# Four-layer graph network: the second edge order made by a top-eight sort on VectorE, with fewer scatters

## The chip, the cores and the metric

One core of a Trainium2 chip. The metric is the device time of one execution in microseconds, the median of several runs. Engines by their short names: PE is TensorE, DVE VectorE, ACT ScalarE, POOL GpSimd, SP SyncE, which here issues plain DMAs only.

## What is computed

Four graph layers on 3125 nodes of 256 features (padded to 3200, 25 blocks of 128) and 103125 edges (padded to 128 partitions x 806), each layer added to x and followed by a layer norm. Cut to what matters:

```python
x = _layernorm(x + _L0_gnn_ref(x, edge_index, edge_attr_2, ...))
x = _layernorm(x + _L1_gnn_ref(x, W_self, W_neigh, src, dst))
x = _layernorm(x + _L2_gnn_ref(x, Wf, Wb, loop_weight, ..., src, dst, edge_type_16, 0, 0))
x = _layernorm(x + _L3_gnn_ref(x, edge_index, ...))
...
# in _L1_gnn_ref
h_sparse = _maxk(feat @ W_neigh, 32)
summed = segment_sum(h_sparse[src], dst, num_segments=n)
return feat @ W_self + summed / maximum(deg, 1.0)[:, None]
...
# in _L2_gnn_ref, for (src, dst) and again for (dst, src)
proj = einsum('ni,rio->rno', feat, W)
m = (proj[etypes, src_idx] + bias) * norm_per_edge[:, None]
m_out = segment_sum(m, dst_idx, num_segments=n)
...
# in gt_layer of _L3_gnn_ref, twice: rows are src, cols are dst
att = clip(einsum('ehd,ehd->eh', q, k), -10.0, 10.0)
attNorm = segment_sum(exp(att), rows, num_segments=n)[rows]
```

The edges come sorted by dst. Layers 0, 1 and the forward half of layer 2 sum over dst; the backward half of layer 2 and both attention passes of layer 3 sum over src, and need the edges in a second order, by block of src (src // 128).

## The kernel before

**Edge sums.** Edges stand in 832 tiles of 128 in SBUF, each tile with nodes of one block only: `slots_d` (by dst) and `slots_s` (by src, three words an edge: node, relation row, place in the block). Every pass over the edges takes the tiles in 208 groups of four. ACT writes the four columns of row numbers (`gidx`, four slots in a ring), POOL issues four indirect DMAs that gather 128 table rows each (`gather_loop`, L233), DVE writes the one-hot matrices (`one_hot`, L242), PE multiplies them by the rows (`sum_tile`, L273), and DVE adds the four results to the block's sums (`adder`, L261). ACT may write slot n only when the sums of group n - 4 are done, so POOL runs at most four groups ahead. Stages in order, with the names used here:

- e0, layer 0 (L558 to L648), then norm n0; d1, layer 1's dense part, with a top-32 of each row by MAX8 and MATCH_REPLACE8 (L1195, L1198) and table1 stored;
- e1, layer 1's edge sum, then norm n1; d2, the dense part of layer 2;
- pf, the projections of 16 relations to `table2f` (PE L1436, DVE L1284, SP stores L893); e2f, its edge sum, with the backward projections beside it (from `rel_res`, loaded by SP at its start, L816, in eight pairs);
- e2b over `slots_s`, then layer 3: e3a and e3b over `slots_s`.

**The second order.** A counting sort spread over the program. `sort_keys` (L396 to L406) forms keys and records before e0. In e0, DVE counts the edges of each block between groups (`count_bin`, L411), `sort_tiles` (L443 on) makes the block starts, and `rank_bin` (L418 to L425) gives the first 208 edge columns a row each, one block of src after every fourth group. In e1 the other 598 columns are ranked in the same way. The rows are then used by `scatter` (L500 to L513): POOL copies 13 columns of records and rows to a stage buffer, then issues 13 indirect DMAs, each writing 128 records of three words to `slots_s_dram`. 208 of the 806 scatters follow e0's gathers on POOL's queue, 598 follow e1's, ahead of e2f's:

```python
            gather_loop(pool, "e0", table0, 2 * ROW0)
            pool.wait_ge(sem("gs_rows"), 1)
            scatter(pool, "gs", slots_s_dram, rec_s, row_s, 0, NS_EARLY)
            ...
                gather_loop(pool, "e1", table1, C)
                pool.wait_ge(sem("gs_moved"), 1)
                pool.wait_ge(sem("gs_rows"), 2)
                scatter(pool, "gs", slots_s_dram, rec_s2, row_s2, NS_EARLY, NS)
                for s in range(2):
                    pool.wait_ge(sem(f"pf_stored{s}"), 32 * PAIRS * (NB // 5) // 2)
                gather_loop(pool, "e2f", table2f, C)
```

SP waits for all of them after six of the eight pairs of relation weights (L527) and loads `slots_s` back.

## Time and profile before

| | us |
|---|---|
| median of 3 runs (9871.92 to 9894.19) | 9883.51 |
| span of the profiled execution, first to last instruction | 7939.2 |
| busy: POOL / PE / DVE / ACT | 5744.1 / 4723.0 / 4571.4 / 1304.4 |
| mean granted TensorE clock, share of full | 0.790 |

The profile gives the profiled execution's span alone, not a time of its own with what lies around it; the runs' median is 1944.3 us longer than the span. A POOL indirect DMA is busy while POOL writes its descriptors; the data lands later.

### The profile page before, as it was taken

The page shows a single profiled execution, that of the slowest core. Times are in us where ns is not written, and L with a number is a line of the kernel's source. Part 1 is how long each engine was busy: PE and PEld are TensorE (multiplying, and loading weights), DVE is VectorE, ACT ScalarE, POOL GpSimd, SP SyncE. Part 2 cuts the span into 40 slices and gives each one's busy share as a digit, 9 for nine tenths or more (in the row PEclk, how much of TensorE's full clock was granted, in tenths as well). Part 3 has the DMA queues.
Part 4 walks back from the last instruction along what each step waited for, and adds up shares of the span by engine and source line. Part 5 has one row for each costly group of instructions (what it writes and reads, how often), then busy time and mean ns, then how long its engine had stood idle before and what let it go on. Part 6 is the DMA issues. An engine that isn't in the chain of part 4 may idle for free.

```text
span 7939.2 us, 105932 instructions
## 1 busy us (share of the span) xinstructions
PE 4723.0 (59%) x17448; PEld 3281.5 (41%) x17449; DVE 4571.4 (58%) x11380; ACT 1304.4 (16%) x5226; POOL 5744.1 (72%) x5938
## 2 busy tenths in 40 slices
PE   4555653355555890077777556655666665666664
PEld 3333431233333440044444334433555554555553
DVE  6788887355444440055555544444666666666666
ACT  4666650000000000000000000001211111111111
POOL 4777777777777777777777777774677774777773
PEclk7777676677777995599999776676888887888887
DMA  3332330233333351055555333332333333333332
GB/s 100 56 57 55 57 50 21 66 97 98 101 103 87 117 161 31 23 149 157 158 157 158 100 102 103 102 103 67 101 102 101 101 102 80 100 101 100 101 101 64
DMA packets 513845, 751.71 MB, mean 95 GB/s; under 512 B 232770, under 2 KB 365943, under 8 KB 513271
## 3 DMA queue, kind: packets, MB, share of 16 engines
q0 software_dynamic: 252096, 604.80, 28.1%
q1 hardware_dynamic: 261686, 146.25, 6.1%
q8 instruction: 18, 0.29, 0.0%
q14 instruction: 45, 0.36, 0.0%
HBM read 624.19 MB, written 126.41 MB: 95 GB/s over the span
## 4 chain that ended last, share of the span: by engine, by line
POOL 51%; issue 35%; DMA 5%; ACT 3%; DVE 2%; PE 2%; POOLq 1%; ACTq 0%; DVEq 0%; SPq 0%
POOL rows L233 41%; POOL slots_s_dram L513 10%; DMA rows<-table,gidx 3%; ACT msg L577 2%; PE ps L273 1%; ACT big L565 1%; PE ps L359 1%; DMA rows<-table2f,gidx 0%; DVE big L671 0%; DMA rows<-table3b,gidx 0%; DMA rows<-table3a,gidx 0%; POOLq L77 0%; DMA rows<-table2b,gidx 0%; DVE x_sb L680 0%; DVE acc L261 0%
## 5 line engine op out<-in xcount | busy, mean ns | idle before, releaser
L261 DVE TENSOR_TENSOR acc<-acc,ps 128x257 f32 (+3 forms) x4992 | 1879.7, 377 | 1980.8 <-PE ps L273 1788.6
L273 PE MATMUL ps<-rows,onehot 128*128 128x257 f32 (+1 forms) x4992 | 1689.7, 498 | 1664.6 <-DMA rows<-table2f,gidx 602.2
L273 PEld LDWEIGHTS ps<-rows,onehot 128*128 128x128 f32 x4992 | 1162.6, 244 | 2277.8 <-issue 1711.8
L233 POOL DMA_INDIRECT rows<-table,gidx x1664 | 1647.6, 990 | 512.7 <-issue 458.7
L273 PE MATMUL ps<-msg,onehot 128*128 128x136 f32 (+1 forms) x4992 | 1282.9, 418 | 536.9 <-ACT msg L577 345.6
L273 PEld LDWEIGHTS ps<-msg,onehot 128*128 128x128 f32 x4992 | 981.6, 253 | 835.1 <-issue 378.6
L233 POOL DMA_INDIRECT rows<-table3a,gidx x832 | 820.9, 987 | 362.4 <-issue 251.3
L233 POOL DMA_INDIRECT rows<-table3b,gidx x832 | 829.3, 997 | 333.2 <-issue 251.3
L233 POOL DMA_INDIRECT rows<-table2b,gidx x832 | 821.2, 987 | 269.1 <-issue 251.6
L513 POOL DMA_INDIRECT slots_s_dram<-stage,stage_row x806 | 798.7, 991 | 274.4 <-issue 226.9
L233 POOL DMA_INDIRECT rows<-table2f,gidx x832 | 788.6, 948 | 253.4 <-issue 253.4
L776 DVE TENSOR_TENSOR big<-ps,rows 128x512 f32<-128x512 f32 x416 | 287.8, 692 | 724.3 <-DMA rows<-table3b,gidx 363.4
L735 PE MATMUL ps<-ident,onehot 128*128 128x128 f32 x1664 | 310.2, 316 | 543.4 <-DVE onehot L242 538.1
L744 PE MATMUL ps<-acc,msg 128*128 x3328 | 564.6, 324 | 80.9 <-issue 78.0
L744 PEld LDWEIGHTS ps<-acc,msg 128*128 128x128 f32 x3328 | 517.6, 236 | 129.1 <-issue 127.9
L223 ACT ACTIVATE gidx<-slots_d 128x4 int32 (+1 forms) x416 | 85.9, 208 | 2851.2 <-PE ps L273 2851.2
L735 PEld LDWEIGHTS ps<-ident,onehot 128*128 128x128 f32 x1664 | 196.0, 153 | 627.3 <-DVE onehot L242 535.9
L242 DVE TENSOR_TENSOR onehot<-iota,slots_s 128x512 f32<-128x512 f32 x624 | 430.2, 690 | 0.7 <-DVE acc L1317 0.2
L577 ACT ACTIVATE msg<-big,msg 128x64 f32<-128x64 f32 x1664 | 419.8, 334 | 6.8
L703 ACT ACTIVATE gidx<-slots_s 128x4 int32 (+1 forms) x416 | 85.5, 206 | 1762.8 <-DVE msg L797 1762.8
L1436 PE MATMUL ps<-wring,big 128*128 128x512 f32 x800 | 346.5, 597 | 7.9 <-DMA wring<-in_rel_f 7.9
L1453 PE MATMUL ps<-big,xts 128*128 128x512 f32 x600 | 285.2, 598 | 22.3 <-ACT xts L1036 22.3
...
## 6 DMA issues: line engine op xcount, KB each, us to landing
...
table2b<-msg SPq DMA_DIRECT2D x200, 256.0 KB, 2.3
rows<-table,gidx POOLq DMA_INDIRECT x1664
slots_d<-recs_d SPq DMA_DIRECT2D x832, 2.5 KB
rows<-table2f,gidx POOLq DMA_INDIRECT x832
rows<-table2b,gidx POOLq DMA_INDIRECT x832
rows<-table3a,gidx POOLq DMA_INDIRECT x832
rows<-table3b,gidx POOLq DMA_INDIRECT x832
```

The source lines that it names most:

```text
L223: nc.scalar.activation(gidx[:, h, :], src_ap[:, :, word], ACT.Copy).then_inc(sem("row_numbers"), 1)
L233: nc.gpsimd.indirect_dma_start(out=rows[:, j, 0:width], out_offset=None, in_=table[:, :], in_offset=bass.IndirectOffsetOnAxis(ap=gidx[:, h ...
L242: nc.vector.tensor_tensor(onehot[:, h, :, :], bc(iota[:, :].unsqueeze(1), [P, G, P]), bc(loc, [P, G, P]), ALU.is_equal).then_inc(sem(of(s, ...
L261: nc.vector.tensor_tensor(acc[:, bass.ds(b * width, width)], acc[:, bass.ds(b * width, width)], ps[:, bank + k, 0:width], ALU.add).then_in ...
L273: nc.tensor.matmul(ps[:, bank + k, 0:width], onehot[:, h, k, :], rhs, start=True, stop=True).then_inc(sem(of(s, "tile_sum")), 1)
L513: nc.gpsimd.indirect_dma_start(out=dram_slots[:, :], out_offset=bass.IndirectOffsetOnAxis(ap=stage_row[:, h, k:k + 1], axis=0), in_=stage[ ...
L577: last = nc.scalar.activation(msgA[:, h, k, a * F0:(a + 1) * F0], ms0[:, h, k, 0:F0], ACT.Copy, scale=msgA[:, h, k, HEADS * F0 + a:HEADS * ...
L735: last = nc.tensor.transpose(ps[:, h % 2, k * P:(k + 1) * P], onehot[:, h, k, :], ident[:, :])
L744: last = nc.tensor.matmul(ps[:, 2 + h % 2, k * D:(k + 1) * D], oneT[:, h, k, :], q_sb[:, bass.ds(b * D, D)], start=True, stop=True)
L776: nc.vector.tensor_tensor(qk3[:, h, :, :], ps[:, 2 + h % 2, :].rearrange("p (g d) -> p g d", d=D), rows4[:, h, :, 0:D], ALU.mult).then_inc ...
L1436: last = nc.tensor.matmul(ps[:, m % 5, :], xt_all[:, k, m * P:(m + 1) * P], wring[:, s, k, :], start=(k == 0), stop=(k == 1))
L1453: last = nc.tensor.matmul(ps[:, 4 + q % 4, :], xts[:, 0, k * P:(k + 1) * P], rel_res[2 * q + k], start=(k == 0), stop=(k == 1))
```

## The change

The second order is made during e1. SP loads src, dst and edge type after layer 1's weights. DVE packs each edge in one 32-bit word (63 - block of src, dst, place, type; `pack_codes`), and takes the eight largest of a partition's 808 words at a time (`top_of`, `less_top`): three rounds in every four groups, 34 times, so that each partition's words are sorted by block. The sorted words are cut in 202 chunks of four; the words of chunks that mix blocks are sorted once more on their own, in 14 rounds (112 words). `count_codes` and `code_rows` compare all 202 chunks (and 112 singles) with the 25 blocks in one instruction each to count them and to look up their rows. POOL then places 202 chunks and 112 single words (the compiled program has 112, the change's name 104) in `codes`, right from SBUF. Before e2f, SP loads `codes` tile by tile, PE transposes seven pieces, and DVE decodes them to `slots_s`. The sort's work before and in e0 goes, with all scatters after e0.

```diff
+    CHUNK = 4
+    NCH = -(-EC // CHUNK)
+    SW = NCH * CHUNK
+    SORT_IT = -(-SW // 24)
+    NSG = -(-((BINS + 1) * CHUNK) // 8) * 8
+    SORTED = 24 * SORT_IT
+    COUNTED = -(-(4 * (SORT_IT + 1) + 2 + NSG // 8 + 2) // 4) * 4
     KD, KS = 5, 3
...
+        def pack_codes(dve, link):
+            dve.wait_ge(sem("gs_loaded"), 16 * 3)
+            flip = (FULL_KEY << 7) & ~(P - 1)
+            link(nc.vector.memset(left[:, EC:SW], LOWEST))
+            link(nc.vector.tensor_scalar(part_i, src_i, P - 1, 4, ALU.bitwise_and, ALU.logical_shift_left))
+            link(nc.vector.tensor_scalar(src_i, src_i, flip, flip, ALU.bitwise_xor, ALU.bitwise_and))
+            link(nc.vector.scalar_tensor_tensor(part_i, src_i, KEY_BIT - 7, part_i, ALU.logical_shift_left, ALU.bitwise_or))
+            link(nc.vector.scalar_tensor_tensor(part_i, dst_i, 12, part_i, ALU.logical_shift_left, ALU.bitwise_or))
+            link(nc.vector.tensor_tensor(left[:, 0:EC].bitcast(i32), part_i, et_i, ALU.bitwise_or))
+            dve.sem_inc(sem("gs_replaced"), 1)
...
+        def top_of(dve, r, steps):
+            after(dve, "gs_replaced", steps + 1)
+            dve.nop(nofuse=True)
+            nc.vector.max(top8[:, r, :], left).then_inc(sem("gs_top"), 1)
+        def less_top(dve, r, steps):
+            after(dve, "gs_top", steps + 1)
+            dve.nop(nofuse=True)
+            nc.vector.match_replace(left, top8[:, r, :], left, LOWEST).then_inc(sem("gs_replaced"), 1)
...
+        def count_codes(dve, bins, eq, counts, width, link):
+            link(nc.vector.tensor_tensor(eq, bc(iota[:, 0:NB].unsqueeze(2), [P, NB, width]),
+                                         bc(bins.unsqueeze(1), [P, NB, width]), ALU.is_equal))
+            link(nc.vector.tensor_reduce(counts[:, 0:NB], eq, AX.X, ALU.add))
...
+        def code_rows(dve, bins, eq, table, before, look, pos, junk, to, width, link):
+            link(nc.vector.tensor_tensor(eq, eq, bc(table[:, 0:NB].unsqueeze(2), [P, NB, width]), ALU.mult))
+            link(nc.vector.tensor_reduce(look, eq.rearrange("p s c -> p c s"), AX.X, ALU.add))
+            link(nc.vector.scalar_tensor_tensor(junk, bins, float(NB), to, ALU.is_ge, ALU.mult))
+            link(nc.vector.scalar_tensor_tensor(pos, bins, float(NB), before, ALU.is_lt, ALU.mult))
+            link(nc.vector.tensor_tensor(pos, pos, look, ALU.add))
+            link(nc.vector.tensor_tensor(to, pos, junk, ALU.add))
...
+        BATCH = 16
...
+        def place_codes(pool):
+            single_rows = codes.rearrange("r (w a) -> (r w) a", a=1)
+            for i in range(NCH + NSG):
+                n = i // BATCH
+                if i % BATCH == 0:
+                    after(pool, f"gs_placed{n % 2}", 16 * BATCH * (n // 2))
+                if i < NCH:
+                    rows_out, at, what = codes, to_c[:, i:i + 1], kept[:, i * CHUNK:(i + 1) * CHUNK]
+                else:
+                    j = i - NCH
+                    rows_out, at, what = single_rows, to_s[:, j:j + 1], singles[:, j:j + 1]
+                nc.gpsimd.indirect_dma_start(
+                    out=rows_out[:, :], out_offset=bass.IndirectOffsetOnAxis(ap=at, axis=0), in_=what, in_offset=None,
+                ).then_inc(sem(f"gs_placed{n % 2}"), 16)
+        def codes_placed(eng):
             for h in range(2):
-                sp.wait_ge(sem(f"{o}_placed{h}"), SC_EDGES * 8 * NS)
-            sp.dma_start(slots[:, :], dram_slots.rearrange("(p t) w -> p (t w)", p=P)).then_inc(sem(o + "_slots"), 16)
...
-            sp.wait_ge(sem("gd_done"), 1)
-            weight(key_i, edges(src), "gs_loaded")
-            weight(other_i, edges(dst), "gs_loaded")
-            weight(etype_i, edges(etype), "gs_loaded")
...
+                weight(src_i, edges(src), "gs_loaded")
+                weight(dst_i, edges(dst), "gs_loaded")
+                weight(et_i, edges(etype), "gs_loaded")
...
-                        slots_load(sp, "gs", slots_s_dram)
+                        codes_placed(sp)
+                        tiles = codes.rearrange("r w -> (r w)")[0:T * P].rearrange("(t p) -> t p", p=P)
+                        full_t = T // P * P
+                        weight(codes_t[:, 0:T // P, :], tiles[0:full_t, :].rearrange("(k t) p -> t k p", t=P), "codes_loaded")
+                        weight(codes_t[0:T - full_t, T // P, :], tiles[full_t:T, :], "codes_loaded")
...
                     pool.wait_ge(sem(f"gd_placed{h}"), SC_EDGES * 8 * NS)
             pool.sem_inc(sem("gd_scattered"), 1)
-            pool.wait_ge(sem("gs_keyed"), 1)
+            pool.wait_ge(sem("gd_done"), 1)
             pool.memset(acc[:, :], 0.0).then_inc(sem("acc_clear"), 1)
+            pool.wait_ge(sem("attr_ranged"), 1)
...
-            pool.wait_ge(sem("gs_rows"), 1)
-            pool.wait_ge(sem("gs_filled"), 16)
-            scatter(pool, "gs", slots_s_dram, rec_s, row_s, 0, NS_EARLY)
...
             if layers > 1:
+                pool.wait_ge(sem("e0_done"), 1)
+                pool.iota(to_c, [[P, NCH]], base=TRASH_C // CHUNK, channel_multiplier=1).then_inc(sem("gs_trash"), 1)
+                pool.iota(to_s, [[P, NSG]], base=TRASH_S, channel_multiplier=1).then_inc(sem("gs_trash"), 1)
                 pool.wait_ge(sem("d1_stored"), TABLE_STORED)
                 gather_loop(pool, "e1", table1, C)
-                pool.wait_ge(sem("gs_moved"), 1)
+                pool.wait_ge(sem("gs_filled"), 16)
                 pool.wait_ge(sem("gs_rows"), 2)
-                scatter(pool, "gs", slots_s_dram, rec_s2, row_s2, NS_EARLY, NS)
+                pool.nop(nofuse=True)
+                place_codes(pool)
...
-            sort_keys(dve, "gs", link)
-            dve.sem_inc(sem("gs_keyed"), 1)
...
-            for n in range(R):
-                step(n, n)
-            with dve.Fori(0, NB) as b:
-                for h in range(R):
-                    step(b * R + (R + h), h)
-                count_bin(dve, "gs", b)
-            count_bin(dve, "gs", NB)
-            sort_tiles(dve, "gs", link)
-            with dve.Fori(0, NB) as b:
-                for h in range(R):
-                    step(b * R + ((NB + 1) * R + h), h)
-                rank_bin(dve, "gs", b, EARLY, sem("gs_rank"))
-            rank_bin(dve, "gs", NB, EARLY, sem("gs_rank"))
...
                 dve.wait_ge(sem("block_ev"), first["d1"] + NB)
-                nc.vector.tensor_copy(rec_s2, rec_s).then_inc(sem("gs_moved"), 1)
...
+                pack_codes(dve, link)
...
+                def group(n, h, begin=plain, end=plain):
+                    later = not isinstance(n, int) or n > 0
+                    if later:
+                        add = adder(dve, "e1", block_d, n - 1, 0, C + 1)
+                        add(0)
+                    after(dve, "tile_sum", tiles0["e1"] + G * (n - R + 1))
+                    one_hot(dve, "e1", slots_d, KD, n, h)
+                    begin(n)
+                    if later:
+                        for k in range(1, G - 1):
+                            add(k)
+                    end(n)
+                    if later:
+                        add(G - 1)
+                for n in range(R):
+                    group(n, n)
+                with dve.Fori(0, SORT_IT) as i:
+                    for h in range(R):
+                        if h < 3:
+                            group(i * R + (R + h), h, lambda n: top_of(dve, h, i * 3 + h), lambda n: less_top(dve, h, i * 3 + h))
+                        else:
+                            group(i * R + (R + h), h)
+                            nc.vector.tensor_copy(kept[:, bass.ds(i * 24, 24)].rearrange("p (r w) -> p r w", r=3), top8[:, 0:3, :])\
+                                .then_inc(sem("gs_kept"), 1)
+                            dve.wait_ge(sem("gs_kept"), i + 1)
+                n = R * (SORT_IT + 1)
+                dve.wait_ge(sem("gs_replaced"), 3 * SORT_IT + 1)
...
+                mixed_chunks(dve, link)
+                n += 2
+                for k in range(NSG // 8):
+                    steps = 3 * SORT_IT + k
+                    group(n, n % R, lambda n: top_of(dve, 0, steps), lambda n: less_top(dve, 0, steps))
+                    nc.vector.tensor_copy(singles[:, k * 8:k * 8 + 8], top8[:, 0, :]).then_inc(sem("gs_kept"), 1)
+                    dve.wait_ge(sem("gs_kept"), SORT_IT + k + 1)
+                    n += 1
...
+                    .then_inc(sem("gs_ge"), 1)
+                group(COUNTED + 6, (COUNTED + 6) % R)
+                dve.wait_ge(sem("gs_trash"), 2)
+                code_rows(dve, bin_c, eq_c, tab_c, upto, look_c, pos_c, junk_c, to_c, NCH, link)
+                dve.sem_inc(sem("gs_rows"), 1)
+                group(COUNTED + 7, (COUNTED + 7) % R)
+                code_rows(dve, bin_s, eq_s, tab_s, iota[:, 0:NSG], look_s, pos_s, junk_s, to_s, NSG, link)
+                dve.sem_inc(sem("gs_rows"), 1)
...
+                for half in range(2):
+                    link(nc.vector.tensor_copy(block_s[0:1, half * (T // 2):(half + 1) * (T // 2)], ps[0:1, 6 + half, 0:T // 2]))
+                rest = -(-(COUNTED + 9) // R)
...
                 link(nc.vector.tensor_copy(deg.unsqueeze(2), a1[:, :, C:C + 1]))
                 link(nc.vector.reciprocal(small[:, 160:160 + NB], small[:, 160:160 + NB]))
                 link(nc.vector.tensor_tensor(a1[:, :, 0:C], a1[:, :, 0:C], bc(small[:, 160:160 + NB].unsqueeze(2), [P, NB, C]), ALU.mult))
                 link(nc.vector.tensor_tensor(x3, x3, a1[:, :, 0:C], ALU.add))
-                dve.wait_ge(sem("gs_moved"), 1)
-                for h in range(2):
-                    dve.wait_ge(sem(f"gs_placed{h}"), SC_EDGES * 8 * NS_EARLY)
                 norm_dve(dve, "n1", x3, C, 1e-5, link)
                 dve.sem_inc(sem("e1_done"), 1)
                     dve.wait_ge(sem(f"pf_stored{s}"), 32 * PAIRS * (NB // 5) // 2)
                 dve.sem_inc(sem("pf_done"), 1)
                 link(nc.vector.memset(acc[:, :], 0.0))
+                dve.wait_ge(sem("codes_turned"), 1)
+                loc_i, node_i, type_i = decoded
+                for a, b, bank in ((0, 512, 5), (512, T, 6)):
+                    raw = ps[:, bank, 0:b - a].bitcast(i32)
+                    link(nc.vector.tensor_scalar(loc_i[:, a:b], raw, 4, 2 * P - 1, ALU.logical_shift_right, ALU.bitwise_and))
...
```

POOL's program from the end of e1's gathers to the start of e2f's. Before (L233 is a gather, L505 and L508 the stage copies, L513 the scatters; ISA rows are waits):

```order
L233 DMA rows<-table,gidx 128x256 x16
L520 UNCONDITIONAL_BRANCH
L520 ISA
L505 ISA
L505 COPY stage<-msg 128x39
L508 ISA
L508 COPY stage_row<-msg 128x13
L510 ISA
L513 DMA slots_s_dram<-stage,stage_row 106624x3 x13
```

Now (L252 is a gather, L645 the scatters):

```order
L71 COMPARE_AND_BRANCH
L252 DMA rows<-table,gidx 128x256 x16
L645 DMA codes<-msg 56064x4 x202
L645 DMA codes<-msg 224256x1 x112
L252 DMA rows<-table2f,gidx 128x256 x16
L71 UNCONDITIONAL_BRANCH
```

The stage copies and two loops of 13 scatters, run 46 times in all, have become 314 single scatters in a row.

DVE in e1's loop, at the end of a turn of four groups. Before (L261 adds a tile's sum, L418 to L425 rank one block):

```order
L261 ISA
L261 TENSOR_TENSOR acc<-acc,ps 128x257
L71 REGISTER_ALU
L261 ISA
L261 TENSOR_TENSOR acc<-acc,ps 128x257
L418 ISA
L418 TENSOR_SCALAR big,cnt<-big,iota 128x598
L421 SCALAR_TENSOR_TENSOR big<-big 128x598
L423 REGISTER_ALU
L423 SCALAR_TENSOR_TENSOR big<-big,base 128x598
L425 TENSOR_TENSOR big<-big 128x598
```

Now, within one group (L261 writes the one-hots, L280 adds a sum, L514 and L520 are a round of the sort):

```order
L261 TENSOR_TENSOR onehot<-iota,slots_d 128x512
L65 ISA
L514 MAX top<-big 128x8
L65 REGISTER_ALU
L280 ISA
L280 TENSOR_TENSOR acc<-acc,ps 128x257
L65 REGISTER_ALU
L280 ISA
L280 TENSOR_TENSOR acc<-acc,ps 128x257
L520 MATCH_REPLACE big<-top,big 128x808
L65 REGISTER_ALU
L280 ISA
L280 TENSOR_TENSOR acc<-acc,ps 128x257
```

The ranking after every fourth group is gone, and MAX and MATCH_REPLACE over 808 words stand between the additions of three groups in four.

## Rows read from the trace of the kernel before

**Rows 1.** The page: the chain of work that ended last, by engine and by line.

```profile
POOL 51%; issue 35%; DMA 5%; ACT 3%; DVE 2%; PE 2%; POOLq 1%; ACTq 0%; DVEq 0%; SPq 0%
POOL rows L233 41%; POOL slots_s_dram L513 10%; DMA rows<-table,gidx 3%; ACT msg L577 2%; PE ps L273 1%; ACT big L565 1%; PE ps L359 1%; DMA rows<-table2f,gidx 0%; DVE big L671 0%; DMA rows<-table3b,gidx 0%; DMA rows<-table3a,gidx 0%; POOLq L77 0%; DMA rows<-table2b,gidx 0%; DVE x_sb L680 0%; DVE acc L261 0%
```

**Rows 2.** Busy time by stretch: stretch and length, engines, granted clock, DMA share and GB/s.

```profile
core 0: us, PE busy (x) PEld busy (x) DVE busy (x) ACT busy (x) POOL busy (x), PEclk, DMA share, GB/s
...
97.00:1165.00 1068.00, 616.30 (x1653) 417.06 (x1654) 868.17 (x2720) 678.09 (x2874) 808.72 (x833) 0.74 0.31 56
1165.00:1455.00 290.00, 83.85 (x180) 37.83 (x178) 164.17 (x480) 27.61 (x92) 219.12 (x241) 0.64 0.09 16
1455.00:2548.00 1093.00, 625.56 (x1648) 425.00 (x1648) 554.90 (x1164) 42.44 (x204) 839.60 (x834) 0.72 0.35 99
...
2640.00:2991.00 351.00, 345.13 (x799) 152.42 (x797) 138.47 (x200) 0.00 (x0) 261.22 (x307) 0.99 0.51 160
2991.00:3353.00 362.00, 0.00 (x0) 0.00 (x0) 6.25 (x2) 0.00 (x0) 268.90 (x315) 0.50 0.05 10
3353.00:4395.00 1042.00, 764.21 (x2438) 451.63 (x2439) 589.52 (x1227) 52.83 (x231) 788.61 (x832) 0.98 0.53 156
```

**Rows 3.** POOL in order of time at the handovers: start, duration, what, idle before.

```profile
1455.67 1.00 POOL L233 DMA_INDIRECT rows<-table,gidx  x1 [0.30 <-issue]
...
2547.00 0.94 POOL L233 DMA_INDIRECT rows<-table,gidx  x1 [0.30 <-issue]
...
3351.90 0.95 POOL L513 DMA_INDIRECT slots_s_dram<-stage,stage_row  x1 [0.30 <-issue]
3353.16 0.99 POOL L233 DMA_INDIRECT rows<-table2f,gidx  x1 [0.30 <-issue]
```

**Rows 4.** POOL by line: count, busy us, mean ns, idle before.

```profile
L513 POOL DMA_INDIRECT slots_s_dram<-stage,stage_row x806 | 798.7, 991 | 274.4 <-issue 226.9 <-POOL stage_row L508 47.5
L233 POOL DMA_INDIRECT rows<-table2f,gidx x832 | 788.6, 948 | 253.4 <-issue 253.4
```

**Rows 5.** DVE in order of time: end of layer 0, table 1 stored, projections stored.

```profile
1185.03 0.43 DVE L261 TENSOR_TENSOR acc<-acc,ps 128x260 f32 x1 [0.21 <-DVE acc L261]
...
1371.12 5.56 DVE L1213 MEMSET acc<- 128x6600 f32 x1 [3.30 <-issue]
...
2992.89 5.56 DVE L1297 MEMSET acc<- 128x6600 f32 x1 [7.02 <-issue]
```

**Rows 6.** POOL before its first gather.

```profile
91.83 5.60 POOL L977 MEMSET acc<- 128x6600 f32 x1 [80.55 <-DVEq L1114]
```

**Rows 7.** A stretch of layer 1 after its ranking, columns as in rows 2.

```profile
2100.00:2500.00 400.00, 236.50 (x627) 159.49 (x627) 171.94 (x391) 16.23 (x78) 304.98 (x313) 0.72 0.35 102
```

**Rows 8.** DVE by line and shape: count, busy us, mean ns, idle before.

```profile
L1195 DVE MAX8 top<-msg 128x8 f32<-128x256 f32 x75 | 32.1, 428 | 7.7
L1198 DVE MATCH_REPLACE8 msg<-top,msg 128x256 f32<-128x256 f32 x75 | 30.7, 409 | 0.5 <-issue 0.3
...
L411 DVE TENSOR_SCALAR_CACHE_REDUCE big<-big,iota 128x806 f32<-128x806 f32 x26 | 27.2, 1047 | 0.2 <-DVE big L411 0.2
L418 DVE TENSOR_SCALAR_CACHE_REDUCE big<-big,iota 128x598 f32<-128x598 f32 x26 | 21.6, 829 | 0.2 <-DVE big L425 0.2
```

**Rows 9.** POOL scatters beside MAX8 work of DVE, and beside its wide additions.

```profile
1251.06 0.96 POOL L513 DMA_INDIRECT slots_s_dram<-stage,stage_row  x1 [0.30 <-issue]
...
2561.79 6.73 POOL L513 DMA_INDIRECT slots_s_dram<-stage,stage_row  x1 [0.30 <-issue]
```

**Rows 10.** DVE beside that long scatter.

```profile
2560.86 6.82 DVE L1236 TENSOR_TENSOR acc<-acc,small 128x6400 f32<-128x6400 f32 x1
```

**Rows 11.** SP's queue after the projections, and what the DMA engines moved from 2990 to 3040.

```profile
2991.81 6.22 SPq L816 DMA_DIRECT2D big<-in_rel_b  x12
...
GB/s 199 8 84 139 348 373 356 354 349 351 261 13 1 1 1 0 1 1 1 1 1 1 1 1 1 1 1 1 1 0 1 1 1 1 1 1 1 1 1 1
```

**Rows 12.** PE by line: the transposes by the identity.

```profile
L735 PE MATMUL ps<-ident,onehot 128*128 128x128 f32 x1664 | 310.2, 316 | 543.4 <-DVE onehot L242 538.1 <-issue 5.2
```

375 lines of the change are left out of this document (236 added, 139 removed).

## The prediction

> **What bounds the kernel now.** First I read the page's chain of waits [rows 1]. POOL carries 51% of it, and the 35% called issue are nearly all the gaps between POOL's own instructions, so read them as POOL's too. By line it is the gathers, 41%, and the scatters of the second order, 10%. Then the busy times by stretch [rows 2]: in no stretch but the projections (2640 to 2991, PE 345 of 351 us) does another engine fill its time. In 2991 to 3353 PE is idle and DVE busy 6 of 362 us: everybody waits for POOL's scatters. In 1165 to 1455 DVE is done with layer 0 and the top-32 long before POOL is free. The handovers on POOL's queue give the exact times [rows 3]: the gathers of e1 run from 1455.67 to 2547.94, the 598 late scatters up to 3353, and only then e2f's gathers begin. Last I read what else had to be ready at those handovers [rows 5]: table 1 was stored at 1371.1, where the clearing of the sums is released, and the last projections at about 2991.4 (1.5 us before the second clearing, which waits for them and starts at 2992.89; SP's next load, behind the same wait, was issued just before the ones at 2991.81 [rows 11]). So POOL is late by 84.6 us at e1 and by 361.8 us at e2f. That is the reach of this change; what is beyond it belongs to the gathers.
>
> **The change, part by part.** The sum is made against the profiled span, 7939.2 us. The runs' median is 9883.5, 1944.3 us more; I take that difference as fixed, and come back to it as a rival.
>
> *Before e0.* POOL's first gather waits for its clearing of the sums, which waited till 91.83 for the keys of the second order [rows 6]. Now it waits for the first order only, done some 12 us earlier by the three loads and seven DVE instructions that go (SP's loads of those words no longer stand ahead of the record loads either): -12, with bounds of -5 (only DVE's work goes) and -13.
>
> *e0.* 832 gathers take from 97 to 1165, 1.28 us each. DVE is busy 868 of 1068 us and loses about 27 us of counting (26 of 1.05 us [rows 8]) and the ranking of 208 columns. POOL's own pace hardly depends on it: I take 7 us for the stop at `sort_tiles` and small waits (0 to 15). DVE's last sum stands at 1185.0 [rows 5], 20 us after the last gather, part of it behind the last ranking: -5 (0 to -10).
>
> *Early scatters.* 208 scatters go. What is late next is table 1: the dense part and top-32 are a chain of their own from the end of e0. So e1's gathers start when the table is stored: -84.5. The bound on the other side is -80, if three more SP loads of 400 KB delay the weights.
>
> *e1.* The gathers took 1092.3 us. After its ranking POOL does 313 in 400 us [rows 7], 1.278 each, so 832 would be 1063. Into this DVE now gets 116 rounds of the sort. The shapes of 598 and 806 columns [rows 8] differ by 1.05 ns an element; MAX8 of 256 takes 428 ns and MATCH_REPLACE8 409, so 808 elements make 1.01 and 0.99 us, with 0.1 for loading the eight values 2.1 us a round. DVE's busy time after the ranking is 172 us in 400, 2.2 a group; with a round 4.3 us, and a group has 5.1. It fits, and since the order of additions is kept and POOL may run four groups ahead, I cost the sorting loop at nothing. The work at its end doesn't fit: compares and look-ups over 5050 and 2800 elements, by the wide addition of 6400 in 6.82 us [rows 10] 5.4 and 3.0 us each, four pairs of them in all, with small operations 10.8, 6.0, 12.5 and 7.3 us, and 5 us for the block tables, between seven groups or so. DVE behind by L gains back 1.6 us a group; POOL's lead forgives about 9. Going through them in order, 4, 6 and 6 us are left over: +17. Bounds are 0 and all 42. e1 is then 1080 us, -12 (from -50, at e2f's pace of 1042 for 832 [rows 2] and no stall, to +13).
>
> *Late scatters.* 598 scatters took 805 us, 1.345 each with the copies. The new 314 need no copies: 0.96 + 0.30 us [rows 9] = 1.26, or 397 us, and the two wide additions of the norm, beside which the one at 2561.79 took 6.73 instead of 0.96, add 11.5: 408 us. From the end of e1's gathers to the projections' store are 443.5 us. The cover is the projections, PE-bound and untouched. Even at the old 1.345 + 11.5 the 314 end in 434. So the scatters cost nothing, and e2f starts with the projections: -361.8.
>
> *Before e2f.* New in front of DVE's first one-hot: `codes` comes behind 12 weight loads, which keep the DMA engines at some 350 GB/s till 3003 [rows 11], so about 3005; seven transposes at two instructions of 0.316 us [rows 12] under 4.5 us; nine decodes of 2496 + 2496 elements at 1.05 ns and some 0.15 each, 6.6 us. DVE begins near 3015, not 2998. POOL meanwhile issues its four groups (20 us) and would stand from 3011 to about 3020: +9 (0 to +25). The last four weight loads wait behind the codes, but are needed eight groups later.
>
> Sum: -12 - 7 - 5 - 84.5 - 12 - 361.8 + 9 = **-473.3**, a span of 7466 and a time of 9410. All bounds on one side give 9349 and 9475.
>
> **A rule against the rows.** The scatter at 2561.79 was held for as long as an addition of two SBUF operands ran [rows 9, 10], while scatters beside MAX8 took 0.96 [rows 9]; I price the four wide compares as such holds, partly hidden in the 17 us. The Trainium skill ("SBUF — State Buffer", Who interferes with whom) says that tensor_tensor takes only the shared pair's read side, which descriptor writing does not need, though it holds up GpSimd instructions that read SBUF; an indirect DMA reads its row numbers there. By its first half the compares would cost POOL nothing and the placing 11.5 us less: by that rule e1 would be some 5 us shorter, and the hidden placing would only be better hidden. That sentence moves the sum to 9405 and no chance.
>
> **The rivals.**
>
> *The sort makes DVE the bound of e1* (0.11). If MAX8 and MATCH_REPLACE8 grow in proportion to width, a round is (428 + 409 + 92) x 808/256 = 2.9 us and a group 5.1, its whole period: then nothing is gained back, the 42 us of bursts show in full and each round costs perhaps 0.4 more, 46 us. 25 + 46 more than my 17: 9481. For it speaks that only one width of both is in the trace; against it that their 428 and 409 ns are what an addition of 256 takes, and that one grows by 1.05 ns an element.
>
> *The scatter of four costs like four* (0.02), the case slower than before. If POOL wrote a descriptor per word, 202 x 4 + 112 = 920 at 1.26 us and 11.5 make 1173 us against 443.5: 730 us more than the sum, a time of 10140. The point from which the change loses is a placing of 443.5 + 473 = 917 us, or 3.8 us for a scatter of four. Against it: a gather of 256 words takes 948 ns and a scatter of three words 991 [rows 4]; width has no price there.
>
> *What lies around the span scales with it* (0.06). Then the time falls by 473.3 x 9883.5 / 7939.2 = 589, to 9294. Nothing in the profile shows what the 1944 us are; work outside the first and last instruction has no reason to know of scatters.
>
> *The change doesn't do what it says, or another wait takes its place* (0.03): the placing waits for its own completions every 16 scatters, or the rows of the chunks come too late. At 1.8 us each it takes 577 us, 133 more than the cover: 9543.
>
> **How the numbers follow.** My case has the remaining 0.78, the forecast is its sum, 9410. Its own bounds are 9349 to 9475, and the first rival lies at 9481. A range of 9355 to 9505 holds both but for their tails, and leaves out the far cases (0.11), which is within 2 in 10. Faster by over 0.2% (20 us, what a measurement here can tell from no change) is all but the slow rival: 0.97; slower 0.02, same 0.01.
>
> **What would show it.** In the profile after: the first gather near 86; e1's first gather right at the clearing of the sums, near 1347; 808-wide MAX8 near 1.0 us, e1's gathers in 1065 to 1100 us with the loss in one place, at the wide compares; 314 scatters in about 408 us, the last one some 35 us before the projections' last store; e2f's first gather near 2871, with one stand of POOL of about 9 us after 16 gathers; everything after it unchanged, 4595 us from that gather to the end (4586 before, and that stand). I am wrong if the scatters of four are longer than those of one, if DVE has no idle time in e1, if PE idles between projections and e2f by more than 30 us, or if the time falls by a different amount than the span.

## The result

The kernel after takes 9426.88 us (median of 4 runs, 9384.17 to 9436.32), before 9877.88: a ratio of 0.953 [0.951, 0.955], 451 us less. Forecast were 9410 and a range of 9355 to 9505. The number is close; the working is not. The first line of the profile after says so:

```profile
span 9434.5 us, 105027 instructions
## 1 busy us (share of the span) xinstructions
PE 5082.2 (54%) x17459; PEld 3439.7 (36%) x17460; DVE 4737.4 (50%) x11500; ACT 1337.1 (14%) x5226; POOL 5238.6 (56%) x5323
...
another core or an unknown queue 11%; PE 10%; issue 5%; DVE 5%; DVEq 2%; POOL 1%; DMA 0%; ACT 0%; SPq 0%; POOLq 0%; ACTq 0%
```

This execution took 9436.32 us, so only 1.8 us lie outside its span. I had put 1944 us there. And POOL, 51% of the chain before [rows 1], has 1% of it now. That is not the change's doing: a profile of the kernel before with a time near 9870 (the next section) gives POOL 0%. The shares of such a chain add up to a third of the span only, so I read nothing else from it. The stretches between POOL's handovers, from the windows of the profile after (columns as in [rows 2]):

```profile
core 0: us, PE busy (x) PEld busy (x) DVE busy (x) ACT busy (x) POOL busy (x), PEclk, DMA share, GB/s
86.62:1480.10 1393.48, 582.15 (x1638) 401.98 (x1638) 811.76 (x2517) 683.03 (x2872) 816.67 (x832) 0.71 0.23 43
1480.10:1682.80 202.70, 82.70 (x185) 36.93 (x185) 158.97 (x486) 28.88 (x97) 0.47 (x3) 0.72 0.10 27
1682.80:2996.60 1313.80, 710.59 (x1672) 362.98 (x1672) 742.04 (x1491) 42.45 (x204) 821.23 (x832) 0.68 0.29 83
2996.60:3421.30 424.70, 63.96 (x160) 41.98 (x158) 61.57 (x160) 17.81 (x55) 320.65 (x314) 0.52 0.03 3
3421.30:3795.60 374.30, 346.37 (x800) 153.00 (x800) 140.32 (x206) 0.00 (x0) 0.04 (x1) 0.96 0.45 152
3795.60:9434.50 5638.90, 3263.52 (x12830) 2418.53 (x12830) 2766.06 (x6542) 540.63 (x1893) 3266.03 (x3328) 0.72 0.30 90
```

Row 1 is e0: 832 gathers in 1393 us, 1.68 us each, though POOL is busy as long per gather as before (816.67 / 832 = 0.98 us). Rows 4 and 5 are the surprise: the 314 scatters take 424.7 us, about the 408 forecast, but beside them TensorE is busy 64 us and not one of the 800 products of the projections is made. They all follow in row 5, in 346 us. The scatters were placed under a cover, and the cover all but stopped while they ran. The clock is not the reason: TensorE's granted clock was 0.52 in row 4, near the lower of its two levels (1.2 GHz), but it sat idle for 361 of the 424.7 us.

### The profile page after: what moved, and what is told of

The parts are those of the page before. It is cut to its first block and busy times, and to the rows that moved or that the text cites. A ratio compares the mean times of both kernels' runs of the same rounds, so it can differ in the third digit from the quotient of the medians.

```text
span 9434.5 us, 105027 instructions
## 1 busy us (share of the span) xinstructions
PE 5082.2 (54%) x17459; PEld 3439.7 (36%) x17460; DVE 4737.4 (50%) x11500; ACT 1337.1 (14%) x5226; POOL 5238.6 (56%) x5323
## 5 line engine op out<-in xcount | busy, mean ns | idle before, releaser
L280 DVE TENSOR_TENSOR acc<-acc,ps 128x257 f32 (+3 forms) x4992 | 1884.2, 377 | 2387.9 <-issue 1012.9
L292 PE MATMUL ps<-rows,onehot 128*128 128x257 f32 (+1 forms) x4992 | 1866.5, 513 | 1547.1 <-DVE onehot L261 624.1
L252 POOL DMA_INDIRECT rows<-table,gidx x1664 | 1637.9, 984 | 1212.2 <-issue 505.1
L292 PEld LDWEIGHTS ps<-rows,onehot 128*128 128x128 f32 x4992 | 1097.9, 244 | 2374.3 <-issue 1289.7
L292 PEld LDWEIGHTS ps<-msg,onehot 128*128 128x128 f32 x4992 | 1039.2, 269 | 1087.1 <-issue 905.1
L252 POOL DMA_INDIRECT rows<-table2f,gidx x832 | 796.0, 957 | 855.3 <-DMA table2f<-big 374.3
L252 POOL DMA_INDIRECT rows<-table3a,gidx x832 | 823.5, 990 | 690.2 <-ACT gidx L827 308.6
L252 POOL DMA_INDIRECT rows<-table3b,gidx x832 | 823.5, 990 | 650.9 <-ACT gidx L827 288.0
L252 POOL DMA_INDIRECT rows<-table2b,gidx x832 | 823.0, 989 | 443.3 <-issue 255.6
L868 PE MATMUL ps<-acc,msg 128*128 x3328 | 643.7, 355 | 469.4 <-issue 265.3
L868 PEld LDWEIGHTS ps<-acc,msg 128*128 128x128 f32 x3328 | 580.3, 262 | 532.9 <-issue 532.5
L859 PE MATMUL ps<-ident,onehot 128*128 128x128 f32 x1664 | 385.0, 375 | 699.4 <-DVE onehot L261 598.6
L261 DVE TENSOR_TENSOR onehot<-iota,slots_s 128x512 f32<-128x512 f32 x624 | 431.1, 691 | 553.4 <-remote 494.8
L859 PEld LDWEIGHTS ps<-ident,onehot 128*128 128x128 f32 x1664 | 268.9, 193 | 761.6 <-DVE onehot L261 522.6
L378 PE MATMUL ps<-wring,xts 128*128 128x256 f32 (+4 forms) x550 | 214.0, 518 | 365.6 <-issue 300.0
L645 POOL DMA_INDIRECT codes<-msg x314 | 320.7, 1021 | 104.0 <-issue 103.7
L1650 PE MATMUL ps<-big,xts 128*128 128x512 f32 x600 | 329.8, 678 | 83.9 <-ACT xts L1163 74.0
L1625 PE MATMUL ps<-wring,big 128*128 128x512 f32 x800 | 346.4, 596 | 23.4 <-DMA wring<-in_rel_f 23.4
```

The lines of the kernel that those rows point to most:

```text
L252: nc.gpsimd.indirect_dma_start(out=rows[:, j, 0:width], out_offset=None, in_=table[:, :], in_offset=bass.IndirectOffsetOnAxis(ap=gidx[:, h ...
L261: nc.vector.tensor_tensor(onehot[:, h, :, :], bc(iota[:, :].unsqueeze(1), [P, G, P]), bc(loc, [P, G, P]), ALU.is_equal).then_inc(sem(of(s, ...
L280: nc.vector.tensor_tensor(acc[:, bass.ds(b * width, width)], acc[:, bass.ds(b * width, width)], ps[:, bank + k, 0:width], ALU.add).then_in ...
L292: nc.tensor.matmul(ps[:, bank + k, 0:width], onehot[:, h, k, :], rhs, start=True, stop=True).then_inc(sem(of(s, "tile_sum")), 1)
L378: last = nc.tensor.matmul(ps[:, 2 + j, 0:wide], xts[:, j, k * P:(k + 1) * P], weights[:, k, 0:wide], start=(k == 0), stop=(k == kin - 1))
L645: nc.gpsimd.indirect_dma_start(out=rows_out[:, :], out_offset=bass.IndirectOffsetOnAxis(ap=at, axis=0), in_=what, in_offset=None,).then_in ...
```

## The experiments

### The kernel before, once more

Unchanged, to have a profile of an execution whose time is known. 

> The kernel before, unchanged, to get a profile of an execution whose time is known. Theory A (the missing 1944 us lie inside the loops; the profile shown of before was of a quicker execution): the span is the time less about 2 us, near 9876, with e0's gathers at about 1.68 us each and e2f's at about 1.54, as in the profile after, and the stage d2 slow as there (about 380 us). Theory B (they lie outside the span): a span near 7939 beside a time near 9880, e0 at 1.28 and e2f at 1.25 us a gather. If A holds, this run also gives the two stands before e1 and before e2f in such an execution; theory A1 has them at about 85 and 362 us as in the profile before, theory A2 (d2 is slow too, so that the projections end some 800 us after e1) has the second near zero, and most of the 451 us must come from somewhere else.

Measured: 9870.62 us (before in this series, with the next two runs: 9873.01), the profiled span 9848.0. Windows of its profile:

```profile
97.70:1499.40 1401.70, 557.32 (x1640) 383.26 (x1641) 878.28 (x2701) 679.82 (x2865) 811.28 (x833) 0.72 0.23 43
1499.40:1874.20 374.80, 98.18 (x193) 43.01 (x191) 162.85 (x495) 30.06 (x101) 216.89 (x240) 0.60 0.06 12
1874.20:3119.60 1245.40, 644.88 (x1652) 397.45 (x1652) 570.85 (x1165) 42.44 (x204) 831.20 (x832) 0.67 0.31 87
3119.60:3966.10 846.50, 248.17 (x375) 101.96 (x374) 98.02 (x215) 17.81 (x55) 602.01 (x690) 0.55 0.08 18
3966.10:4230.00 263.90, 255.56 (x588) 112.41 (x588) 104.70 (x152) 0.00 (x0) 0.00 (x1) 0.98 0.49 164
```

Theory A holds: 1.8 us lie outside the span, and every stretch up to e2f's first gather is longer than in [rows 2]. The three stretches without gathers that come later (e2f to e2b, e2b to e3a, e3a to e3b) are not: 15.4, 110.2 and 79.4 us here, 16.0, 109.3 and 80.0 in the profile that I worked from. From e1's last gather to e2f's first are 1110.4 us, not 805, and after the scatters TensorE still has 588 of its 800 products to do. Neither A1 nor A2 foresaw this.

### The kernel before without its 806 scatters

```diff
-            scatter(pool, "gs", slots_s_dram, rec_s, row_s, 0, NS_EARLY)
...
-                scatter(pool, "gs", slots_s_dram, rec_s2, row_s2, NS_EARLY, NS)
...
```

> The kernel before without its 806 scatters of the second order (208 after e0, 598 after e1) and without the waits for them; sorting and ranking stay. It leaves out the placing of the second order, so e2b and the attention layers gather row 0 throughout. Theory 1 (what POOL stands for after e0 and after e1 is worth what the profile before shows): 85 + 362 = 447 us less than before, about 9431, up to the start of e2f's gathers, and later stages may differ by gathering one row. Theory 2 (in an ordinary execution the second layer's dense part is so slow that the late scatters are nearly hidden already): e2f's first gather comes only some 100 us earlier. Theory 3 (the scatters themselves slow the dense part and the others beside them): more than 447 us, since the dense part gets back to 50 us.

Measured: 9144.48 us, 0.926 [0.925, 0.928], 729 us less. The two stretches of its profile:

```profile
1499.40:1705.50 206.10, 84.52 (x193) 38.09 (x193) 164.70 (x502) 29.74 (x101) 0.00 (x0) 0.72 0.08 20
2949.30:3391.60 442.30, 385.17 (x973) 182.58 (x972) 203.57 (x374) 17.39 (x55) 0.04 (x1) 0.93 0.40 131
```

Theory 3. Without scatters the second stretch is 442.3 us, what I had worked out for it (443.5). So 208 early scatters cost 374.8 - 206.1 = 169 us of the 298 they take, and 598 late ones 1110.4 - 442.3 = 668 of 846. Later stages gather one row over and over here and are slower for it (e2b 1378 us in place of 1242).

### The kernel after with its scatters issued twice

```diff
...
                 place_codes(pool)
+                codes_placed(pool)
+                place_codes(pool, 1)
```

> The kernel after with its 314 scatters issued twice, the second time after the first has landed. In its profile POOL stood 374 us between the last scatter and the projections. Theory 1 (the placing is hidden work with 374 us to spare, and does nothing to others): the second pass takes 425 us and 5 us of waiting, so 56 us more, about 9483. Theory 3 (the scatters slow the dense part of layer 2, which took 381 us beside them and ended with them): the dense part and the projections after it move little if it would have ended anyway at 3436, again about 56 us more; but if the projections are slowed as well, 100 to 400 us more.

Measured: 9806.14 us, 379 more than after. Windows:

```profile
3040.00:3855.00 815.00, 189.91 (x298) 81.98 (x298) 84.04 (x193) 17.80 (x55) 616.51 (x594) 0.54 0.07 13
3855.00:4164.40 309.40, 285.86 (x652) 125.04 (x652) 115.77 (x168) 0.00 (x0) 0.00 (x0) 0.96 0.45 153
```

The 374 us of POOL's idle time are no reserve. The second pass of some 430 us moves e2f's first gather 369 us later, since beside it TensorE makes only 800 - 652 = 148 products of the projections, 65 us' worth at the speed of the second row. So the projections are held up as well, the case for which 100 to 400 us more were expected.

### A memset in place of each scatter, and scatters from 32 partitions

```diff
-                nc.gpsimd.indirect_dma_start(
-                    out=rows_out[:, :], out_offset=bass.IndirectOffsetOnAxis(ap=at, axis=0), in_=what, in_offset=None,
-                ).then_inc(sem(f"gs_placed{n % 2}"), 16)
+                nc.gpsimd.memset(slots_s[:, 1000:2160], 0.0).then_inc(sem(f"gs_placed{n % 2}"), 16)
+                after(pool, f"gs_placed{n % 2}", 16 * (BATCH * (n // 2) + i % BATCH + 1))
```

> The kernel after with each of its 314 placing scatters replaced by a memset of 128 x 1160 on POOL, about 1 us each, and a wait for it. It leaves the placing of the second order out (codes keep their filling, so e2b and the attention gather row 0). The question is what of the scatters slows the layers' dense part and the projections beside them: in the runs so far the stretch from e1's last gather to e2f's first takes 799 us with 314 scatters, 442 without any. Theory W (the writing of descriptors, or their DMAs, holds up TensorE): 442 us, so about 9070. Theory B (POOL being busy at all, for 400 us, holds up the others): 799 again, about 9430.

```diff
-                    rows_out, at, what = codes, to_c[:, i:i + 1], kept[:, i * CHUNK:(i + 1) * CHUNK]
+                    rows_out, at, what = codes, to_c[0:32, i:i + 1], kept[0:32, i * CHUNK:(i + 1) * CHUNK]
```

(and the same for the single words). 

> The kernel after with its 314 scatters writing the rows of 32 partitions only, a quarter of the descriptors each. It leaves out three quarters of the placing. Theory W1 (the hold grows with descriptors or with POOL's time in the instruction): the scatters take less than their 0.97 us, 0.4 to 0.6, and the stretch from e1's last gather to e2f's first falls from 799 to about 442 + 357/4 to 442 + 357/2, 530 to 620 us. Theory W2 (each indirect DMA costs the others the same, whatever its size): about 800 again. Theory 0 (the DMA engines' small writes are the hold): they are a quarter, so about 530, with scatters as long as before.

Measured: 9286.58 and 9392.22 us, on another chip, where before takes 9829.99. The stretch from e1's last gather to e2f's first decides. With memsets, first their line in the profile (ns: least, median, most), then the windows:

```profile
L645 POOL MEMSET slots_s<- x314: 1065/1065/1117, 2938.5 to 3310.4; 128x1160 f32 x157
...
2938.50:3311.50 373.00, 300.10 (x776) 145.28 (x777) 193.56 (x322) 17.40 (x55) 334.63 (x315) 0.90 0.35 116
3311.50:3400.40 88.90, 82.05 (x192) 36.02 (x190) 33.59 (x49) 0.00 (x0) 0.02 (x2) 0.98 0.47 161
```

With scatters from 32 partitions:

```profile
L645 POOL DMA_INDIRECT codes<-msg x314: 856/865/6667, 2955.2 to 3370.4; - x157
...
2954.90:3371.30 416.40, 53.92 (x124) 32.63 (x125) 60.56 (x144) 13.44 (x40) 314.78 (x315) 0.50 0.03 3
3371.30:3766.50 395.20, 358.55 (x849) 162.24 (x847) 148.39 (x230) 4.14 (x15) 0.01 (x1) 0.95 0.43 144
```

POOL busy for 335 us with memsets leaves TensorE 300 us of work in 373, and the stretch is 461.9 us. Indirect DMAs of a quarter of the rows take 0.87 us in place of 0.97 and leave it 54 us in 416; the stretch is 811.6. So theory W, in the form W2: what holds the others up comes with the indirect DMA, not with POOL's work, and hardly depends on how many rows it moves. Its price is (811.6 - 442.3) / 314 = 1.18 us each. With 128 rows it is (799.0 - 442.3) / 314 = 1.14 on the first chip; on this one the next two runs have stretches of 808.2 and 809.4 us, 1.17 each. In time the whole for memsets misses its 9070, since e2b and the attention gather one row (e2b 1426 us).

### The large sort ahead of e1

```diff
+                with dve.Fori(0, SORT_IT) as i:
+                    for h in range(R):
+                        if h < 3:
+                            top_of(dve, h, i * 3 + h)
+                            less_top(dve, h, i * 3 + h)
...
                 with dve.Fori(0, SORT_IT) as i:
                     for h in range(R):
...
-                            group(i * R + (R + h), h, lambda n: top_of(dve, h, i * 3 + h), lambda n: less_top(dve, h, i * 3 + h))
+                        group(i * R + (R + h), h)
```

> The kernel after with the 102 rounds of the large sort (MAX8 and MATCH_REPLACE8 of 808) run in one piece ahead of e1's first group on DVE, no longer inside its groups. In the runs so far e1's gathers take 1314 us with the sort inside and 1245 without. Theory S (the rounds inside the loop cost the 69 us, since DVE's part of each group is on the ring of waits, while the bursts at the wide compares cost little): the rounds alone take 102 x 2.1 = 214 us ahead, and the groups then run at 1.497 us a gather, so e1 ends 214 - 69 = 145 us later, less four groups' lead: 9550 to 9575. Theory L (the 69 us are the wide compares, look-ups and the 14 small rounds, and the 102 rounds cost nothing inside): 200 to 215 us more, 9630.

Measured: 9559.91 us, 0.973 [0.971, 0.976] of before. Its windows, POOL's stand during the sort and then e1 with POOL's lead used up:

```profile
1649.80:1893.20 243.40, 4.83 (x11) 3.87 (x12) 208.31 (x335) 0.21 (x1) 0.00 (x0) 0.50 0.00 1
1893.20:3120.50 1227.30, 651.62 (x1652) 374.22 (x1650) 539.56 (x1131) 42.22 (x203) 807.48 (x816) 0.67 0.31 87
```

From e1's first gather to its last are 1491.3 us (1629.3 to 3120.5); with the sort inside, the three other runs on this chip have 1308.3 to 1324.4. The rounds alone take 247 us (1640.3 to 1887.2), not 214, and moving them costs 167 to 183, so inside the loop they had cost 64 to 80. That is theory S, with the rounds mis-sized. That the time falls in its range is luck: the range was built on the first chip's 9427 us, and on this one a kernel as fast as after takes 9375 (the next run).

### e2b on eight PSUM banks

```diff
-                    sum_tile(pe, s, n, h, k, 0, G, width, rows[:, h * G + k, 0:width])
+                    wide = s == "e2b"
+                    sum_tile(pe, s, n, h, k, h % 2 * G if wide else 0, 2 * G if wide else G, width, rows[:, h * G + k, 0:width])
...
-                    add = adder(dve, s, block, n - 1, 0, width)
+                    add = adder(dve, s, block, n - 1, (h + 1) % 2 * G if s == "e2b" else 0, width)
...
```

> The kernel after with e2b's sums on all eight PSUM banks in turn (banks 0 to 3 for even groups, 4 to 7 for odd) in place of four, so that TensorE may start a group's sums before VectorE has added the last ones'. Theory R (in ordinary executions the gather loops are bound by a ring of waits TensorE - VectorE, lengthened by TensorE's late ends beside POOL's indirect DMAs; 1.497 us a gather where POOL alone would need 1.25 to 1.30): e2b's pace falls to 1.30 to 1.40, 80 to 165 us less, 9260 to 9345. Theory P (POOL's own issue or the landing of the gathered rows bounds the loop): no change beyond 20 us.

Measured: 9374.69 us, 0.954 [0.952, 0.956], as after's 0.953. e2b's gathers take 1229.0 us; with four banks on this chip 1224.7 (the run with 32 partitions) and 1228.4 (sort first). Theory R falls for e2b, the one loop tried: its slower pace does not hang on the banks.

### Three runs that met a quick chip

The next three ran on a chip where the kernel before takes 7941.46 us (7935.36 to 7950.64, 7 runs). That is the kind of execution that the profile before shows. None of them could therefore decide between its theories.

```diff
...
-                        out=rows[:, j, 0:width], out_offset=None, in_=table[:, :],
+                        out=row_tile(h, k)[:, 0:width], out_offset=None, in_=table[:, :],
...
```

(`row_tile` gives the second four groups' rows from `msg`; e2b's loops count modulo eight, and its index waits for the sums of eight groups back.)

> The kernel after with e2b's ring of gathered rows eight groups deep in place of four (the other four in msg, which is free there), everything else of e2b as it was. Eight PSUM banks in place of four changed nothing (e2b 1.478 us a gather before and after). Theory K (late ends of TensorE's products and late register instructions on VectorE, up to 1.4 us each in the trace, are jitter that four groups of lead, 20 us, do not cover): with eight groups POOL hardly waits, 1.28 to 1.35 us a gather, 100 to 165 us less than after. Theory V (the held VectorE sequencer is itself the bound of e2b: its mean need of a group is already 5.9 us): no change beyond 20 us, whatever the ring.

Measured: 7467.03 us, 0.940 of before; e2b 1074.9 us, where the profile of before that I worked from has 1074.3.

```diff
                 pool.wait_ge(sem("gs_rows"), 2)
+                pool.wait_ge(sem("d2_done"), 1)
```

> The kernel after with POOL's 314 scatters held till the dense part of layer 2 is done (one wait more), so that they run beside the projections only. In the runs so far 424 us of scatters let the dense part (50 us alone) just finish. Theory C (what is held is the handing over between engines: the dense part passes each block through TensorE, ScalarE and back, the projections are long runs of products): the projections advance at 30% or more beside the scatters, so that the stretch from e1's last gather to e2f's first is 92 + 424 + 0.7 x 345 minus what ends later, 700 to 760 us in place of 799. Theory E (TensorE's own work is held, whatever it is): the projections advance at some 15 to 25%, 92 + 424 + 260 to 290 = 776 to 806, no gain beyond 25 us.

Measured: 7519.35 us, 0.947 of before. From e1's last gather to e2f's first are 496.6 us, the dense part's 85 and then the scatters' 412. Nothing is held up here, and so neither C nor E is tested. On such a chip the late start costs 37 us (459.5 without it, in the section after this one).

```diff
-                nc.gpsimd.indirect_dma_start(
-                    out=rows_out[:, :], out_offset=bass.IndirectOffsetOnAxis(ap=at, axis=0), in_=what, in_offset=None,
-                ).then_inc(sem(f"gs_placed{n % 2}"), 16)
+                wide = CHUNK if i < NCH else 1
+                first_row = TRASH_C // CHUNK + i * P if i < NCH else TRASH_S + (i - NCH) * P
+                nc.gpsimd.dma_start(rows_out[first_row:first_row + P, 0:wide], what).then_inc(sem(f"gs_placed{n % 2}"), 16)
```

> The kernel after with each of its 314 indirect scatters replaced by an ordinary DMA of the same 128 pieces to fixed rows, still issued by POOL. It leaves the placing out (the words go to rows that nothing reads). Theory W3 (it is the descriptors that POOL writes for an indirect DMA that hold up the others): the stretch from e1's last gather to e2f's first falls to 442 to 500 us unless POOL writes these descriptors too, which would show as about 1 us of POOL's time each. Theory D (the small writes to HBM themselves hold up the others): the stretch stays near 799 us though POOL's time for each falls.

Measured: 8437.19 us. POOL issues an ordinary DMA in 0.54 us and is done with all after 201, yet the stretch is 481 us, 22 more than with the indirect ones on a chip of this kind; no run says why. Whether ordinary DMAs hold the others up on a slow chip stays open. The long time is that of e2b, e3a and e3b, each gathering one row: 1380, 1384 and 1387 us for 1074, 1078 and 1081.

### The kernel after on the quick chip

Unchanged, and beside it the deeper ring again. 

> The kernel after, unchanged. The chips of this study are of two kinds: on two of them the kernel before takes 9830 to 9878 us, on a third 7941, as in the execution whose profile the prediction was made from. Theory Q (on the third kind the prediction's sum of stages holds as it was made, since the scatters hide there): if this chip is of that kind, 7466 us within 10, a ratio of 0.940, with 450 to 455 us from e1's last gather to e2f's first. If it is of the slow kind: a ratio of 0.951 to 0.955 and about 800 us there.

> The kernel with e2b's ring of gathered rows eight groups deep, again, beside the kernel after. On the quick chip POOL's own issue bounded e2b (1.29 us a gather) and the deeper ring gave nothing. Theory K (on a slow chip the holds are jitter that a lead of four groups does not cover): on a slow chip e2b falls from about 1.49 to 1.28 to 1.35 us a gather, 100 to 165 us less than the kernel after. Theory V (VectorE's held sequencer is itself the bound there): less than 20 us. On a quick chip: within 10 us of the kernel after.

Measured: 7484.63 us against before's 7943.82, 0.9421 [0.9405, 0.9437]; the deeper ring 7478.79. The chip is of the quick kind, and theory Q misses its own bounds there, if by little: 7484.63 for 7466 within 10, and 459.5 us from e1's last gather to e2f's first for 450 to 455. The deeper ring's e2b takes 1074.0 us, as after's does, as expected of a quick chip; K against V stays untried on a slow one. Windows of after on this chip, stretch for stretch as above:

```profile
86.70:1130.90 1044.20, 600.03 (x1644) 405.97 (x1645) 796.60 (x2529) 678.02 (x2876) 790.89 (x832) 0.76 0.32 57
1130.90:1332.90 202.00, 85.60 (x181) 37.98 (x179) 155.08 (x473) 27.63 (x92) 0.47 (x2) 0.70 0.11 27
1332.90:2417.50 1084.60, 625.63 (x1664) 420.82 (x1664) 730.19 (x1490) 42.45 (x204) 820.93 (x832) 0.71 0.36 100
2417.50:2841.50 424.00, 362.79 (x910) 173.02 (x910) 190.09 (x350) 17.41 (x55) 316.01 (x314) 0.92 0.52 125
2841.50:2877.00 35.50, 26.59 (x58) 11.13 (x56) 10.95 (x17) 0.00 (x0) 0.00 (x0) 0.89 0.60 154
2877.00:7483.70 4606.70, 2972.42 (x12830) 2184.74 (x12830) 2724.94 (x6542) 514.99 (x1893) 3262.25 (x3328) 0.84 0.38 110
```

Row 4: the same 314 scatters in the same 424 us, and TensorE busy 363 of them where it was 64. This is the cover that I had counted on. The dense part shows the difference in single instructions. VectorE's timeline on the slow chip (start, us, and the idle time before with what ended it):

```profile
3057.21 0.29 DVE L1432 COPY big<-xts 128x256 f32<-128x256 f32 x1 [8.46 <-remote]
3057.42 0.42 DVE L1434 SCALAR_TENSOR_TENSOR big<-ps,bias 128x256 f32<-128x256 f32 x1
3057.87 0.43 DVE L1437 TENSOR_TENSOR x_sb<-x_sb,big 128x256 f32<-128x256 f32 x1
3073.30 0.29 DVE L1432 COPY big<-xts 128x256 f32<-128x256 f32 x1 [15.00 <-remote]
```

and on the quick one:

```profile
2473.70 0.29 DVE L1432 COPY big<-xts 128x256 f32<-128x256 f32 x1 [0.77 <-PE ps L378]
2473.91 0.42 DVE L1434 SCALAR_TENSOR_TENSOR big<-ps,bias 128x256 f32<-128x256 f32 x1
2474.36 0.42 DVE L1437 TENSOR_TENSOR x_sb<-x_sb,big 128x256 f32<-128x256 f32 x1
2474.79 0.35 DVE L1432 COPY big<-xts 128x256 f32<-128x256 f32 x1
```

The instructions are as long; a block of the dense part comes every 10 to 17 us in place of every 1 or 2. In the gather loops the same shows in the register instructions of VectorE's queue. The line of the waits in e2b, on the slow chip (ns: least, median, most):

```profile
L65 DVEq ALU_OP  x927: 1/40/1402, 5203.1 to 6298.8; - x186
L65 DVEq EVENT_SEMAPHORE  x557: 1/21/1399, 5200.3 to 6298.2; - x186
```

and on the quick one:

```profile
L65 DVEq ALU_OP  x978: 40/40/40, 4000.1 to 4999.7; - x196
L65 DVEq EVENT_SEMAPHORE  x586: 21/21/21, 4001.2 to 4999.9; - x196
```

Equal medians, but some of them take 1.4 us where all took 40 or 21 ns.

## Why the prediction was near, and where it was wrong

The terms against both kinds of chip, in us. "Slow" is the kernel after less before in the profiles shown (9434.5 - 9848.0), "quick" after on the quick chip less the profile that I worked from (7483.7 - 7939.2):

| term | forecast | quick | slow |
|---|---|---|---|
| before e0 | -12 | -10.9 | -11.1 |
| e0's gathers | -7 | -23.4 | -8.2 |
| e0's last gather to e1's first | -89.5 | -88.4 | -172.2 |
| e1's gathers | -12 | -7.7 | +68.4 |
| e1's last gather to e2f's first | -361.8 | -345.7 | -311.4 |
| after that | +9 | +20.7 | +20.9 |
| sum | -473.3 | -455.5 | -413.6 |

By medians the slow chips' saving is 451; the 413.6 come from two single executions, before's at the quick end of its runs (9849.82, median 9870.62) and after's the longest of its four.

**The step that failed first** is "I take that difference as fixed". The 1944 us between span and median were not around the kernel but in it: the profile came from a quick chip, the times from a slow one. The rival that looked at this (0.06) let them scale with the span; it fell too, for they are not spread evenly either. What should have made me stop is that a profile and a time 25% apart are two different executions, and a sum made in one is not owed to the other. A sign that I had named came true: the time fell by another amount than the span, which rose from 7939.2 to 9434.5 us while the time fell by 451.

**The scatters cost nothing** was nearly right on the quick chip. The last one ended 35.5 us before e2f's first gather (forecast 35), but both sides of that were 16 us longer than forecast: all 314 took 424 us (408), and the cover 459.5 (443.5). In the cover it was the projections: 359 us from the first product's start to the last's, 346 in the kernel before, with TensorE waiting 8.7 us for VectorE where it had not waited at all, and busy 351.2 for 346.5. No run shows what held VectorE. On the slow chip they cost 357 of their 424.7 us. There my term -361.8 became -311.4, as two errors cancel: the old 598 cost 668 us there, not 362, and the new 314 cost 357, not 0. "Untouched" was the wrong word for the projections.

**Early scatters**: -84.5, or -89.5 with the tail of e0, came out on the quick chip at -88.4. On the slow one 208 of them held up the dense part and the top-32 as well: -172.2. **e0's gathers** were mis-sized: they lost 23.4 us there, for a forecast of 7 and a bound of 15.

**The sort in e1**: MAX8 and MATCH_REPLACE8 of 808 take 996 and 984 ns (forecast 1.01 and 0.99 us), so the first rival's proportional growth is out. The lines of VectorE in e1 on the quick chip:

```profile
L514 DVE MAX8 top<-big 128x8 f32<-128x808 f32 x116 | 115.5, 996 | 0.0
L520 DVE MATCH_REPLACE8 big<-top,big 128x808 f32<-128x808 f32 x116 | 114.2, 984 | 0.0
...
L579 DVE TENSOR_REDUCE big<-big 128x202 f32<-128x5050 f32 x1 | 9.0, 9007 | 0.0
```

One price was wrong, that of the look-up that sums the far axis: 9.0 us for 5.4 over 5050 elements, 4.8 for 3.0 over 2800. e1 took 1084.6 us there (forecast 1080). On the slow chip it took 68.4 more instead of 12 less. That is the first rival's outcome (its 46 us) by another way: not through longer instructions. The run with the sort ahead puts 64 to 80 us on the rounds, enough for all of the 68; that the delays in VectorE's queue leave no room for them in a group is my reading of the lines above, and no run tested it.

**The wide operations** held POOL as the rows before said. POOL's instructions and, below them, VectorE's beside them, on the quick chip:

```profile
2152.92 5.24 POOL L252 DMA_INDIRECT rows<-table,gidx  x1 [0.30 <-issue]
...
2432.02 6.67 POOL L645 DMA_INDIRECT codes<-msg  x1 [0.30 <-issue]
2439.00 6.55 POOL L645 DMA_INDIRECT codes<-msg  x1 [0.30 <-issue]
...
2151.93 5.41 DVE L550 TENSOR_TENSOR big<-iota,big 128x5050 f32<-128x5050 f32 x1
...
2431.02 6.83 DVE L1411 TENSOR_TENSOR acc<-acc,small 128x6400 f32<-128x6400 f32 x1
2437.88 6.82 DVE L1412 TENSOR_TENSOR x_sb<-x_sb,acc 128x6400 f32<-128x6400 f32 x1
```

Each held DMA ends some 0.8 us after VectorE's operation does, near the 0.95 us that one takes undisturbed. (L1411, like L1236 in [rows 10], which the forecast calls an addition, is a product.) Beside the reduction of 9.0 us (2203.23 to 2212.24) POOL's gathers kept to 0.95. The forecast's choice of the rows over a rule of the Trainium skill ("SBUF — State Buffer", Who interferes with whom) stands: that page infers that tensor_tensor takes only the read side of the shared pair and so leaves descriptor writing alone, and these indirect DMAs were held all the same. The page's other rule, that an operation with two inputs in SBUF holds up GpSimd instructions that read SBUF, would fit them, since they read their row numbers there; no run here tells whether it is that read that waits.

**Before e2f** POOL stood 12.1 us after its first 16 gathers (9 forecast), with all that comes after it 11.7 more than the 4595 given.

One reading was too strong and no term hangs on it: the 35% called issue [rows 1] are not nearly all gaps between POOL's instructions, which add up to 1693 us, 21% of the span.

That the total landed near 9410 on a slow chip is luck, by cancellation: 82.7 us more saved between e0's last gather and e1's first, 80.4 less in e1, 50.4 less between e1 and e2f, 11.9 less behind it. The kernel is quicker on both kinds of chip, and its gain on the slow kind has another ground than I gave: 492 indirect DMAs fewer, each of which, at 0.8 to 1.1 us, held up the engines that were to hide it.
